# Context prepared two batches ahead, row centring on GpSimd, and splits moved between VectorE and GpSimd

## The reference, cut to what matters

```python
x = x + _L0_xattn_ref(_layernorm(x, axis=-1), ctx_768, ...)       # 16 heads
x = x + _L0_ffn_ref(_layernorm(x, axis=-1), ...)                  # top 1 of 8 experts: "the routing"
x = x + _L1_xattn_ref(_layernorm(x, axis=-1), ctx_768, ...)       # 8 heads of 64: "the projection" and attention
x = x + _L1_ffn_ref(_layernorm(x, axis=-1), ...)                  # top 8 of 64 experts
...
# inside _L1_xattn_ref
x = stable_layernorm(x, g_norm)
q = jnp.einsum('bnd,de->bne', x, Wq)
kv = jnp.einsum('bmd,de->bme', context, Wkv)
k, v = jnp.split(kv, 2, axis=-1)
...
q = l2norm(q) * q_scale                                           # per head, over 64 columns
k = l2norm(k) * k_scale
```

## Time and profile before

| | us |
|---|---|
| median of 3 runs | 741.32 |
| the runs | 737.27 to 742.46 |
| the profiled execution's own time | 743.77 |
| its span | 742.0 |
| TensorE busy in the span | 652.1 (88%) |
| GpSimd busy in the span | 257.4 (35%) |

### The profile page before, as it was taken

The page is one execution under the profiler, slowest core; times in us unless marked ns, Lnnn a source line. Parts: engine busy times, 40 slices in busy tenths (PEclk is TensorE's granted clock), DMA queues, the critical chain, the costliest instruction groups (busy, mean ns, idle before and its releaser), DMA issues.

```text
span 742.0 us, 15246 instructions
## 1 busy us (share of the span) xinstructions
PE 652.1 (88%) x4810; PEld 520.6 (70%) x4811; DVE 399.2 (54%) x1171; ACT 407.0 (55%) x961; POOL 257.4 (35%) x323
## 2 busy tenths in 40 slices
PE   3998799999799999996877799998597999999995
PEld 2776466666687888974655556666465899999995
DVE  4322577777752111128788645455764666666662
ACT  1444699999755433334556487776341455444442
POOL 5413455555333000013121000000043777777771
PEclk9999799999989999998899999999589899999999
DMA  8118200000284578311110100000005655455552
GB/s 195 50 32 265 76 2 1 2 2 2 58 308 135 168 261 298 108 42 50 31 50 2 49 1 1 2 1 1 14 31 149 180 154 149 145 150 145 144 149 66
DMA packets 73240, 68.10 MB, mean 92 GB/s; under 512 B 13936, under 2 KB 66773, under 8 KB 73062
## 3 DMA queue, kind: packets, MB, share of 16 engines
q1 hardware_dynamic: 68604, 61.02, 27.8%
q0 software_dynamic: 1824, 4.32, 2.3%
q10 hardware_dynamic: 2762, 2.11, 0.9%
HBM read 59.13 MB, written 8.29 MB: 91 GB/s over the span
## 4 chain that ended last, share of the span: by engine, by line
PE 67%; ACT 11%; DVE 11%; issue 4%; DMA 3%; POOL 2%; SPq 1%; ACTq 0%; another core or an unknown queue 0%; DVEq 0%; POOLq 0%
PE psum L791 5%; ACT probs L810 4%; PE psum L1247 4%; PE psum L1234 4%; PE psum L2247 3%; PE psum L2248 3%; PE psum L2249 3%; PE psum L1674 3%; PE psum L2299 3%; PE psum L630 3%; PE psum L1696 3%; PE psum L644 3%; PE psum L1683 3%; PE psum L721 3%; PE psum L1722 2%
## 5 line engine op out<-in xcount | busy, mean ns | idle before, releaser
L810 ACT ACTIVATE probs<-probs,negmax 100x361 f32<-100x361 f32 x128 | 68.9, 587 | 10.1 <-POOL probs L855 10.0
L874 DVE TENSOR_SCALAR_CACHE_REDUCE probs<-psum 100x361 f32<-100x361 f32 x128 | 60.7, 530 | 18.4 <-PE psum L711 18.4
L721 PEld LDWEIGHTS psum<-ident,probs 100*128 100x128 f32 (+1 forms) x384 | 39.7, 157 | 27.0 <-issue 20.0
L721 PE MATMUL psum<-ident,probs 100*128 100x100 f32 (+1 forms) x384 | 48.2, 264 | 11.4 <-ACT probsT L818 4.9
L855 POOL TENSOR_SCALAR probs<-probs 100x722 f32<-100x722 f32 x64 | 50.4, 788 | 5.1
L1274 ACT ACTIVATE kT_all<-psum,qT_all 128x128 f32<-128x128 f32 x88 | 25.0, 369 | 48.2 <-PE psum L1234 48.2
L2247 PE MATMUL psum<-xT_high,we_high 128*128 128x400 f32 x128 | 45.7, 357 | 4.6 <-issue 3.9
L2138 POOL TENSOR_TENSOR xT_low<-kT_all,xT_high 128x1600 fp32r<-128x1600 f32 x1 | 3.6, 3559 | 129.4 <-ACT xT_high L2115 129.4
L2428 POOL TENSOR_TENSOR we_low<-v_all,we_high 128x512 fp32r<-128x512 f32 (+1 forms) x34 | 41.0, 1226 | 15.8 <-ACT we_high L2352 11.3
L1234 PE MATMUL psum<-kT_all 128*128 128x128 f32 x352 | 42.0, 277 | 4.7 <-issue 3.3
L1234 PEld LDWEIGHTS psum<-kT_all 128*128 128x128 f32 x352 | 40.5, 192 | 7.6 <-issue 5.3
(11 more groups left out here) (413 smaller groups left out, 1795.7 us busy)
## 6 DMA issues: line engine op xcount, KB each, us to landing
kT_all<-in_L_ffn_W_dram SPq DMA_DIRECT2D x8, 1024.0 KB, 5.1
kT_all<-coefT_dram SPq DMA_DIRECT2D x18, 400.0 KB, 3.6
qT_all<-in_L_ffn_W_dram SPq DMA_DIRECT2D x12, 512.0 KB, 6.7
ctx_nat<-in_ctx_dram SPq DMA_DIRECT2D x24, 192.0 KB
v_all<-in_L_ffn_Wg_dram SPq DMA_DIRECT2D x34, 128.0 KB, 2.4
v_all<-in_L_ffn_Wu_dram SPq DMA_DIRECT2D x34, 128.0 KB, 2.4
v_all<-in_L_ffn_Wd_dram SPq DMA_DIRECT2D x34, 128.0 KB, 2.4
xs_dram<-zeros SPq DMA_DIRECT2D x1, 2048.0 KB, 7.7
```

The lines of the kernel that those rows point to most:

```text
L721: last = nc.tensor.transpose(pT_ps[0:rows[t], t, hh * NQ:(hh + 1) * NQ], probs[:, n % NPB, hh, t * P:t * P + rows[t]], ident[0:NQ, 0:NQ])
L810: last = nc.scalar.activation(row, row, ACT.Exp, bias=negmax[:, n % NPB, hh:hh + 1])
L874: last = nc.vector.tensor_scalar(probs[:, n % NPB, hh, 0:NKV], psum[0:NQ, n % 2 * 2 + hh, 0:NKV], -CLAMP, None, ALU.max, ALU.max, accum_ou ...
```

## The change

In the routing, `take_ctx1` makes the plain copy for GpSimd only for context 1. VectorE splits context 2 ahead of its wait for the logits and context 3 behind the slots. TensorE finishes the values of batch 0 and transposes context 2 ahead of the last pair of rows, and its two products for the ranks go behind the first tile of batch 1. GpSimd splits context 1 only after seven batches are normalised, and the query weights after its scatters. In the projection, the context is transposed two rounds ahead instead of one. GpSimd centres the rows and multiplies them with `g_norm` (`centre`), in two instructions instead of VectorE's one; statistics are kept for each batch. The factor of the queries is folded into one VectorE instruction of `scale_queries`. Rows are transposed right behind the keys, waiting for the scaled queries of the batch before; VectorE takes them ahead of scaling the keys; query transposes go to bank 6 (to bank 7 for the last batch). In the last round the transposes of the last keys, and ScalarE's copies of them, come behind the queries. Of three pieces the diff shows only the new lines; the old ones stand in the functions above.

```diff
@@ -463,8 +463,12 @@
 
-        return psum[:, (3 * b + t) % 2 + 5, :]
+        return psum[:, t % 2 + 5, :]
     q1_ps = psum[:, 7, :]
+
+    def qT1_ps(b):
+
+        return psum[:, 6 if b < B - 1 else 7, 0:4 * NQ]
 
@@ -985,6 +989,7 @@
         mark(nc.vector.tensor_scalar(block_starts[:, :], iota16[:, 0:MAXB], float(P), None, ALU.mult))
+        split_ctx1(dve, 2)
         dve.wait_ge(gate_loaded, 32)
@@ -1027,6 +1032,7 @@
         nc.vector.tensor_copy(slot[:, :], slot_f[:, :]).then_inc(slots_ready, 1)
+        split_ctx1(dve, 3)
         dve.wait_ge(g_exp, 1)
@@ -1051,16 +1057,17 @@
         take_x(3)
+        take_ctx1(act, 2, False)
         keep_v(act, 0, 2)
-        take_ctx1(act, 2, True)
-        act.wait_ge(g_centred, 1)
-        nc.scalar.activation(logits[:, :, :], logits[:, :, :], ACT.Exp).then_inc(g_exp, 1)
         for b in range(1, B - 1):
             if b == B - 2:
                 act_first_rows(act)
             for t in range(3):
                 keep_v(act, b, t)
-            take_ctx1(act, b + 2, b + 2 <= POOL_CTX)
+                if b == 1 and t == 0:
+                    act.wait_ge(g_centred, 1)
+                    nc.scalar.activation(logits[:, :, :], logits[:, :, :], ACT.Exp).then_inc(g_exp, 1)
+            take_ctx1(act, b + 2, False)
 
@@ -1078,7 +1085,8 @@
         xn_pair(2)
-        early_values(pe, 0, 2, 0, 2)
+        early_values(pe, 0, 2)
+        transpose_ctx1(pe, 2)
         xn_pair(3)
@@ -1087,12 +1095,6 @@
             last.then_inc(gate_logits, 1)
-        early_values(pe, 0, 2, 2, 5)
-        transpose_ctx1(pe, 2)
-
-        pe.wait_ge(choice_ready, 1)
-        nc.tensor.matmul(ranks_ps, earlier[:, :], choice[:, :, :], start=True, stop=True)
-        nc.tensor.matmul(totals_ps, ones_sq[:, :], choice[:, :, :], start=True, stop=True).then_inc(ranks_ready, 1)
         for b in range(1, B - 1):
@@ -1104,16 +1106,16 @@
                 early_values(pe, b, t)
+                if b == 1 and t == 0:
+                    pe.wait_ge(choice_ready, 1)
+                    nc.tensor.matmul(ranks_ps, earlier[:, :], choice[:, :, :], start=True, stop=True)
+                    nc.tensor.matmul(totals_ps, ones_sq[:, :], choice[:, :, :], start=True, stop=True
+                                     ).then_inc(ranks_ready, 1)
         transpose_ctx1(pe, B)
 
     def pool_dispatch(pool):
-        split_ctx1_full(pool, 1)
-        pool.wait_ge(w1x_loaded, 16 * 7)
-        pool.wait_ge(A0.added, B)
-        pool_high(pool, wq1_high, wq1)
-        pool_low(pool, wq1, wq1_high, wq1_low, 7)
-        for n in range(2, POOL_CTX + 1):
-            split_ctx1_full(pool, n)
+        pool.wait_ge(xn_ready, 2 * B - 1)
+        split_ctx1_full(pool, POOL_CTX)
         pool.wait_ge(slots_ready, 2)
@@ -1121,8 +1123,12 @@
                 in_=xn_all[:, b, :], in_offset=None).then_inc(xs_scattered, 16)
-
-    POOL_CTX = 3
+        pool.wait_ge(w1x_loaded, 16 * 7)
+        pool.wait_ge(A0.added, B)
+        pool_high(pool, wq1_high, wq1)
+        pool_low(pool, wq1, wq1_high, wq1_low, 7)
+
+    POOL_CTX = 1
 
@@ -1140,15 +1146,26 @@
         gather(1)
+        def centre(b):
+            pool.wait_ge(x2_step, X2_STEPS * b + X2_STEPS)
+            pool.wait_ge(xnT_in_psum, 2 * B + b)
+            nc.gpsimd.tensor_scalar(xn[:, :], x[:, b + 1, :], mv[:, b, 0:1], None, ALU.subtract).then_inc(xn_centred, 1)
+            pool.wait_ge(xn_centred, b + 1)
+            nc.gpsimd.tensor_tensor(xn[:, :], xn[:, :], g_norm[:, :], ALU.mult).then_inc(xn_ready, 1)
+
         split_ctx1_full(pool, CTX_K[1])
         for b in range(2):
             pool.wait_ge(x2_added, b + 1)
             gather(b + 2)
+            centre(b)
+        split_ctx1_full(pool, CTX_K[2])
         for b in range(2, B):
-            split_ctx1_full(pool, CTX_K[b])
+            if b + 1 < B:
+                split_ctx1_full(pool, CTX_K[b + 1])
             if b + 2 < B:
                 pool.wait_ge(x2_added, b + 1)
                 gather(b + 2)
+            centre(b)
 
@@ -1401,45 +1418,34 @@
         heads = lambda v: v.rearrange("p (h e) -> p h e", e=HD1)
...
+
+        def x_stats(b):
+
+            row, top, mean = x[:, b + 1, :], row_max[:, b:b + 1], mv[:, b, 0:1]
             dve.wait_ge(y_gathered[b % 2], 16 * (b // 2) + 16)
             nc.vector.scalar_tensor_tensor(row, y_tok[:, b % 2, :], top_weight[:, b:b + 1], row, ALU.mult, ALU.add
                                            ).then_inc(x2_added, 1)
             dve.wait_ge(x2_added, b + 1)
             nc.vector.bn_stats(stats[:, 0, :], row).then_inc(x2_step, 1)
...
             dve.wait_ge(x2_step, X2_STEPS * b + 1)
...
+            nc.vector.bn_aggr(mv[:, b, :], stats[:, 0, :]).then_inc(x2_step, 1)
+            nc.vector.tensor_reduce(top, row, AX.X, ALU.max).then_inc(x2_step, 1)
             dve.wait_ge(x2_step, X2_STEPS * b + 3)
...
+            step(dve, nc.vector.tensor_tensor(top, top, mean, ALU.subtract))
+            nc.vector.tensor_tensor(top, top, top, ALU.mult).then_inc(ln_stats, 1)
+
+        def sum_keys(b):
             dve.wait_ge(k1_squared, 2 * b + 1)
             nc.vector.tensor_reduce(key_ss[:, 0:FULL, :], k_sq_full.rearrange("p t (h e) -> p t h e", e=HD1),
                                     AX.X, ALU.add).then_inc(k1_ss, 1)
             dve.wait_ge(k1_squared, 2 * b + 2)
             nc.vector.tensor_reduce(key_ss[0:TAIL, FULL, :], heads(k_sq_tail[0:TAIL, :]), AX.X, ALU.add
                                     ).then_inc(k1_ss, 1)
...
+
+        def scale_keys(b):
+            dve.wait_ge(k1_norm, b + 1)
+            step(dve, nc.vector.tensor_scalar(key_ss[:, :, :], key_ss[:, :, :], 1e-12, None, ALU.max))
+            step(dve, nc.vector.reciprocal(key_ss[:, :, :], key_ss[:, :, :]))
             each = key_ss[:, :, :].unsqueeze(3).broadcast_to([P, 3, 8, HD1])
@@ -1450,8 +1456,11 @@
             nc.vector.tensor_reduce(q_ss[:, :], heads(o_tok[:, :]), AX.X, ALU.add).then_inc(q1_ss, 1)
-            invert(q_ss[:, :], q1_norm, b)
-            step(dve, nc.vector.tensor_scalar(q_ss[:, :], q_ss[:, :], rstd[:, 0:1], None, ALU.mult))
+            dve.wait_ge(q1_norm, b + 1)
+            dve.wait_ge(ln_std, 3 + b + 1)
+            step(dve, nc.vector.scalar_tensor_tensor(q_ss[:, :], std[:, b:b + 1].broadcast_to([NQ, 8]), 1e-12, q_ss[:, :],
+                                                     ALU.mult, ALU.max))
+            step(dve, nc.vector.reciprocal(q_ss[:, :], q_ss[:, :]))
             nc.vector.tensor_tensor(heads(o_tok[:, :]), heads(q1_ps[0:NQ, :]),
@@ -1463,22 +1472,21 @@
 
+        sum_keys(0)
         scale_keys(0)
-        normalised_x(0)
-        x_factor(0)
+        x_stats(0)
+        x_stats(1)
         take_x(0)
-        normalised_x(1)
-        scale_queries(0)
-        x_factor(1)
         for b in range(1, B):
+            sum_keys(b)
+            if b == 1:
+                scale_queries(0)
+            take_x(b)
             scale_keys(b)
-            take_x(b)
-            if b + 1 < B:
-                normalised_x(b + 1)
             scale_queries(b)
             if b + 1 < B:
-                x_factor(b + 1)
-    X2_STEPS = 4
+                x_stats(b + 1)
+    X2_STEPS = 3
 
@@ -1494,8 +1502,10 @@
                 pe.wait_ge(v1_stored, 3 * B - 1 + t)
+            elif t == 1:
+                pe.wait_ge(qT1_stored, b)
             else:
-                pe.wait_ge(kT1_stored, 3 * b + t - 1)
+                pe.wait_ge(kT1_stored, 3 * b + t // 2)
             for c in range(4):
@@ -1503,15 +1513,17 @@
             pe.wait_ge(q1_scaled, b + 1)
+            if b < B - 1:
+                pe.wait_ge(kT1_stored, 3 * b + 2)
             for c in range(4):
-                last = nc.tensor.transpose(q1_ps[:, c * NQ:(c + 1) * NQ], o_tok[:, c * P:(c + 1) * P],
+                last = nc.tensor.transpose(qT1_ps(b)[:, c * NQ:(c + 1) * NQ], o_tok[:, c * P:(c + 1) * P],
                                            ident[0:NQ, 0:NQ])
             last.then_inc(qT1_in_psum, 1)
 
         def x_transposes(b):
             pe.wait_ge(xn_ready, 2 * B + b + 1)
             if b > 0:
-                pe.wait_ge(qT1_stored, b)
+                pe.wait_ge(q1_scaled, b)
             for c in range(2):
@@ -1541,34 +1553,26 @@
             last_values(t)
+        context(2)
         keys(1, range(2))
         x_transposes(0)
         keys(1, (2,))
         queries(0)
...
+        for b in range(1, B):
             if b > 1:
                 keys(b)
...
+            x_transposes(b)
+            for t in range(3):
+                key_transposes(b - 1, t)
             if b > 1:
                 query_transposes(b - 1)
...
+            if b + 2 < B:
+                context(b + 2)
             if b == 1:
                 query_transposes(b - 1)
...
             queries(b)
...
+        for t in range(3):
+            key_transposes(b, t)
         pe.wait_ge(null_k_stored, 1)
@@ -1590,12 +1594,12 @@
             act.wait_ge(ln_stats, 2 * B + b + 1)
```

(26 more changed lines are left out.)

69 lines of the change are left out of this document (2 added, 67 removed).

## The result

The changed kernel takes **744.55 us** (median of 20 runs, 741.33 to 747.30) against 741.27 us for the one before (20 runs, 737.27 to 744.08). The ratio is 1.0043 with a 95% interval of 1.0028 to 1.0059: 3.3 us slower, where 5.6 us of gain were forecast. The profiled execution took 744.62 us, its span 742.8 us. Single executions in the experiments fell in a slower state of the chip: the ratios leave them out, the medians don't.

The account below looks back on a forecast made before the run. TensorE, with 67% of the chain, was taken to bound the kernel through its waits and clock, with DMA second in the routing. Routing 1.9 plus projection 3.7 gave 5.6 us off 741.32: 735.7 us, range 729.5 to 743.5.

Parts of the forecast that it names:

- the slow clock on the new ring: Projection: only short transposes stay on the loop of waits, so a half-clock stretch costs some 0.8 instead of 1.5 us.
- the ring: Projection: loop of waits from one round's key sums to the next; queries and ten key products were to leave it.
- waiting some 3 us for the centred row: Projection: TensorE's wait for GpSimd's row, named among the signs that would show the prediction right.
- signs of being wrong: TensorE never waits for context 4; GpSimd's pair takes over 1.7 us; or projection rounds get no shorter.
- The round at full clock: Projection: one round on the new order takes 10.6 us, with GpSimd's row centred 1.2 us after the key sums start.
- The opening and the end: Projection's start up to the second batch's sums gains 0.9 us; last round up to the first exponential gains 1.6 us.
- The routing: Stage before the experts: gains 1.9 us, with ends of 0.2 and 6.5 us.
- Step 6: Routing: context 4's loads come at 217.3 instead of 218.7, 1.4 us earlier, so its transposes gain 3.6 us.
- The dearer centring: Projection rival: GpSimd's pair keeps VectorE out, losing 0.47 and 0.72 us in each of seven rounds; 744.0 us, chance 0.10.
- its new meeting: Projection: `centre` reads SBUF beside two small two-input VectorE instructions; by the rule each shuts the other out.
- The unchanged clock: Projection rival: the clock stays slow whatever is on the ring, each slow stretch costing 1.5 us; 739.9 us, chance 0.08.

Follow-up runs that it names:

- experiment 3: Changed kernel with the routing as before, so the projection's part of the change alone: 748.82 us, ratio 1.0109 to the kernel before.
- Experiment 4: Changed kernel with TensorE's twelve key transposes moved ahead of the centred row's transposes, GpSimd's pair kept: 724.61 us, ratio 0.9768 to the kernel before.
- experiment 6: Changed kernel, order unchanged, with sixteen useless key transposes in TensorE's wait for the centred row: 737.93 us, ratio 0.9957 to the kernel before.
- experiment 8: Gather behind the centring, first instruction of GpSimd's pair with two tensor operands: 737.14 us on the changed kernel, 725.89 us on that with keys first.
- experiment 7: Context 4 loaded ahead of expert 1's weights: 724.14 us on the kernel with keys first, 741.17 us on the kernel before with the routing's part alone.
- experiment 1: Changed kernel with each row centred and scaled by one VectorE instruction again, instead of GpSimd's pair: 734.60 us, ratio 0.9909 to the kernel before.

## Why the prediction was wrong

**The step that failed** is the slow clock on the new ring: "queries and ten products have left the ring and only the short transposes are on it, so a slow stretch costs some 0.8 instead of 1.5 us". This holds only as long as the clock is full. In experiment 3's round at 1.00 ScalarE squares the queries right behind its other work, and VectorE waits 0.90 us for it, as forecast:

```profile
365.63 0.39 PE L1535 MATMUL psum<-wq_high,xnT_low 128*100 128x512 f32 x1
366.00 0.29 ACT L1595 ACTIVATE std<-row_max,mv 100x1 f32<-100x1 f32 x1
366.18 0.60 ACT L1600 ACTIVATE o_tok<-psum 100x512 f32<-100x512 f32 x1
366.81 0.69 DVE L1456 TENSOR_REDUCE q_ss<-o_tok 100x8 f32<-100x512 f32 x1 [0.90 <-ACT o_tok L1600]
```

But the change put `x_transposes` ahead of `key_transposes`, so TensorE's whole queue from the row's transposes to the queries hangs on the row: 6.9 us in the round at 366.79, 5.9 of them at the low clock. There the queries come too late, ScalarE waits 0.24 us for them and VectorE 2.19 instead of 0.90, and the root is 0.8 us later. The queries are back on the ring. The low clock costs 2.2 us in a round at 0.75 (11.18 against 13.41) and 1.3 in one at 0.86, not 0.8, and it came in all five rounds, behind waits of 2.5 to 3.2 us. The prediction named that wait ("waiting some 3 us for the centred row") as a sign that it was right; it is what brought the low clock. Experiment 4 shortened the wait by the order alone, experiment 6 only filled it; both show it. Of its signs of being wrong two came: rounds got no shorter, and GpSimd's pair took 1.75 us (366.73 to 368.48).

**The round at full clock** was put at 10.6 us and measured 11.18. GpSimd's pair ends 1.69 us after the key sums begin instead of 1.2; with 0.86 the round is 10.49 (experiment 8). This term's mechanism was right, its size 0.5 us short: the first instruction takes 0.94 us, not some 0.5, and the upper end given for the pair, 1.7 us, is about what came.

Together: five rounds were forecast at 56.7 us and took 64.21. The fifth of them has no context to transpose, and took 10.04 us at full clock in experiment 6. So five rounds at full clock are 54.8 us (4 times 11.18, and 10.04), where 53.5 (5 times 10.7) were forecast, 1.3 more; the low clock then costs 9.4 instead of 3.2, 6.2 more. Step by step a round is 9.11 us with the keys first and the earlier row, 10.49 with the row first, 11.18 with the row late, 13.4 with the low clock.

**The opening and the end.** From the first key sums (329.16) to the second round's (354.32) it is 25.16 us, against 25.45 (331.40 to 356.85): 0.3 gained, 0.9 forecast. From the last sums (418.53) to the first exponential (430.24) it is 11.71, against 11.97: 0.3 gained, 1.6 forecast. Both go through the same order: with the keys first they take 23.36 and 10.64 us (experiment 4). Together with the rounds, 7.5 us, this is the 9.4 us between the 3.7 us that the projection was to gain and the 5.7 that it lost in the trace.

**The routing** went nearly as forecast up to context 4: eight quick normalisations, no wait ahead of the gate, slots 7 us earlier, a wait for context 4 with one slow stretch of 3.3 us behind it. Step 6 failed in its time: context 4 was to land 1.4 us earlier with the weights ahead of it and landed no earlier, so TensorE waited 3.87 us instead of 2.9, and 2.2 us are gained up to there instead of 3.6. The scatters that "start 7 us earlier" at no cost now run beside that load. By its interval the routing alone gains 0.5 to 5.0 us, which holds the 1.9 forecast and the 0.6 to 1.1 read from the trace as well. That more of it would come out with context 4 sooner, experiment 7 doesn't bear out.

**The rivals.** The dearer centring gave 744.0, almost the measured time, for another reason than happened. Its price was VectorE being kept out beside GpSimd's pair. By line, to set beside the earlier trace rows:

```profile
L1426 DVE SCALAR_TENSOR_TENSOR x<-probs,top_weight,x 100x256 f32<-100x256 f32 x8 | 4.5, 569 | 0.0
```

The add takes 569 ns in the mean and 476 in the median, against a median of 1242 before, since GpSimd's split of the context is over by then. One tiny instruction beside the pair (L1435) takes 0.36 us, where it takes 0.16 in experiment 1 without the pair, and 0.48 in experiment 8. So the rule of the Trainium skill (SBUF — State Buffer, section Who interferes with whom) had its new meeting, and it was a small term of 0.2 to 0.3 us a round. In experiment 8 the trace agrees with it in full: GpSimd starts first (373.74), and VectorE's instruction ends with GpSimd's, near 374.36. In the changed kernel VectorE starts first (366.51 against 366.73) and is longer all the same, which the first to start holding for its whole length doesn't explain. What made centring dear was who stood behind it in TensorE's order. "The unchanged clock" assumed that a slow stretch costs 1.5 us as now; it had the right subject and two thirds of the price of the long ones.

## What to carry to other kernels

When a result moves to another engine, read the order of the engine that consumes it: what is queued behind the wait pays for the delay, and work that doesn't need the result belongs ahead of it. On TensorE such filling paid twice here, since waits of 2 to 3 us were often followed by half clock just where the ring runs. And when a change "loses", try its order before its placement. With the row first the placement on GpSimd cost 10 us; with the keys first it cost nothing, and that one moved line was worth 20 us.
